# Values of the diagonal key tiles in two parts: the unmasked queries, then the 128 masked ones

## The chip, the cores and the metric

The kernel runs on one core of a Trainium2 chip. The metric is the time of one execution on the device, in microseconds (us). It is the median over several runs.

## What is computed

One transformer block on 2048 tokens of width 128: causal attention with 16 heads of width 8, a LayerNorm, then a feed-forward part with eight experts (each token goes to one) and a shared expert, and a second LayerNorm. The change touches the attention alone:

```python
y = x @ W.T + b                              # q, k, v; 16 heads of width 8
scores = einsum('bhqd,bhkd->bhqk', q, k) * scale
scores = where(k_pos > q_pos, -inf, scores)  # causal
p = softmax(scores - max(scores))
out = einsum('bhqk,bhkd->bhqd', p, v)
x = layernorm(x + out @ Wo.T + bo)
```

## The kernel before

**Tiles.** Queries are taken in four blocks B of 512 (`BLK`), keys in tiles j of 128 (`P`), heads in four groups g of four. A step s = 4B + g is one group of heads on one block of queries. Block B needs the key tiles 0 to 4B + 3. The last four of them, j >= 4B, lie on the diagonal: of tile 4B + d the first 128·d queries of the block see nothing, the next 128 see a triangle, and the rest see all. The first 128·d are never computed (`skip`).

**Two passes.** The *scores* pass finds each query's maximum: TensorE makes products in score_ps (two slots, L1263, and for the diagonal L1270 adds a mask), and VectorE reduces them (L1001). After the last piece of a step comes *maxima*: VectorE takes the maximum over the parts (L1009), GpSimd (POOL) splits it into three bf16 parts in five operations (L747, L752), TensorE turns them (L1278, `maxrows`), ScalarE copies them, and two DMAs lay them into q_stack as an extra row of the product. The second pass works on *quads*, one (g, j) with its four heads. For each quad there are two *probs* items (i = 0 and 1, two heads each): TensorE multiplies keys by queries into ring_ps (L1299), and ScalarE takes the exponential into probs (L876, one instruction a head). On a diagonal tile POOL then sets the forbidden corner of all four heads to zero, in one affine_select on their first 128 columns (L736), and counts `probs_masked` up. Then come the *values*: TensorE multiplies probs by v_aug into out_ps (L1319), which adds up over the key tiles; four matmuls, one a head, side by side in 32 columns of the array each. They are fp32, and the trace has eight records (and eight weight loads) for the four.

**Parts of the values.** The values of a quad can be issued in two parts, `first_values` and `values`. `columns` (L51) says which query columns each takes. Before the change it cuts them in the middle: 256 and 256 of an off-diagonal tile or of j = 4B (d = 0), 192 and 192 for d = 1. The tiles d = 2 (256 columns) and d = 3 (128 columns) are not cut. On a diagonal tile both parts wait for `probs_masked`; elsewhere they wait for `probs_ready`, the exponentials of the four heads.

**What sets the order.** `make_plan` (L61) writes one list of items, and each engine's program goes through it in that order, taking what concerns it. So every engine's queue is in the order of the plan. The second pass gives a fixed sequence (`main`): probs i = 0 of a quad, first_values of the quad before, probs i = 1, values of the quad before. Scores are put between them. The planner keeps a clock for TensorE, VectorE and ScalarE with estimated costs, and puts the next scores when they are due and would stand no longer than the item they go ahead of (L207 to L211). In it `exp_done` is the time at which a quad's probabilities can be used, 750 ns later for diagonal tiles (L171). Once all scores are issued, first_values items are dropped and the values are issued whole (L215). POOL's queue follows the same plan: its five operations of maxima, its masks (at probs i = 1 of the quad) and a `pow` for the LayerNorm (L757, at out_proj) stand there in plan order.

The lines that are spoken of most:

```python
1308                    if j >= TPB * B:
1309                        pe.wait_ge(probs_masked, TPB * s + j - TPB * B + 1)
1310                    else:
1311                        pe.wait_ge(probs_ready, 4 * k + 4)
```

## Time and profile before

| | |
|---|---|
| median of 3 runs | 598.13 us (597.97 to 601.04) |
| the profiled execution, own time | 595.15 us |
| its span, first to last instruction | 593.4 us |
| PE (TensorE matmuls) busy | 529.2 us (89%), 5257 records |
| DVE (VectorE) busy | 454.6 us (77%) |
| ACT (ScalarE) busy | 365.1 us (62%) |
| POOL (GpSimd) busy | 143.2 us (24%) |
| mean granted TensorE clock | 0.966 of full |

Busy time is the time in which an engine has an instruction at work. The profiled execution is a run of its own, 2.98 us below the median. The attention runs from about 22 us (first scores) to 496 us (last values); the last scores are issued at about 437 us. Between 437 and 496 us the second pass ends and is mixed with the first work of the experts; the rest is the experts and the output. "PE" is the matmul, "PEld" the load of its weights; an idle time in square brackets in a timeline row is that of the engine before that row, with what ended it.

### The profile page before, as it was taken

To read this page: it belongs to the slowest core of one execution; us is meant where nothing else is said; L and a number is where in the kernel's file an instruction comes from. 1 tells how busy PE (TensorE), PEld (TensorE's weight loads), DVE (VectorE), ACT (ScalarE), POOL (GpSimd) and SP (SyncE) were. 2 spreads that over 40 slices of the span, in tenths; PEclk is the share of its full clock that TensorE was granted. 3 is DMA by queue.
4 is the path that set the end of the run, shared out by engine and by line. 5 is a ranking of instruction groups with operands and counts; after the bars stand their busy time and mean duration, and the time that the engine had idled before them with its cause. 6 is when DMAs were issued, how large, how long until landed. Compare 5 with 4: busy or idle time off the path is not lost.

```text
span 593.4 us, 14002 instructions
## 1 busy us (share of the span) xinstructions
PE 529.2 (89%) x5257; PEld 218.2 (37%) x5257; DVE 454.6 (77%) x765; ACT 365.1 (62%) x805; POOL 143.2 (24%) x268
## 2 busy tenths in 40 slices
PE   5487899899798999989999999999998999998880
PEld 3243333333333333333333333333324225654460
DVE  4777999899876789888888879879854425777673
ACT  3035676467477666778787877777787984331450
POOL 4633311211201111010101002002013156224744
PEclk9669999899989999999999999999999999999995
DMA  6341002501000420001001000000001012211233
GB/s 152 106 111 54 2 3 58 143 17 31 1 28 2 121 68 2 30 1 29 2 1 29 2 9 21 2 3 2 1 2 36 24 33 56 44 57 34 48 66 93
DMA packets 28882, 22.60 MB, mean 38 GB/s; under 512 B 3528, under 2 KB 28048, under 8 KB 28816
## 3 DMA queue, kind: packets, MB, share of 16 engines
q1 hardware_dynamic: 26848, 18.43, 11.0%
q0 software_dynamic: 1536, 3.15, 3.1%
q8 instruction: 43, 0.70, 0.5%
q14 instruction: 23, 0.19, 0.1%
q10 hardware_dynamic: 432, 0.13, 0.1%
HBM read 8.00 MB, written 4.06 MB: 20 GB/s over the span
## 4 chain that ended last, share of the span: by engine, by line
PE 64%; DVE 12%; issue 6%; ACT 5%; POOL 5%; SPq 4%; DMA 2%; POOLq 0%; DVEq 0%; ACTq 0%
PE out_ps L1319 22%; PE ring_ps L1299 18%; PE score_ps L1263 10%; DVE part_max L1001 6%; SPq L620 3%; ACT probs L876 3%; PE score_ps L1410 3%; POOL probs L736 2%; PE ring_ps L1330 2%; PE ring_ps L1427 1%; PE score_ps L1299 1%; PE score_ps L1270 1%; POOL k_stack L816 1%; PE score_ps L1362 1%; ACT oT L890 1%
## 5 line engine op out<-in xcount | busy, mean ns | idle before, releaser
L1001 DVE TENSOR_REDUCE part_max<-score_ps 128x2 f32<-128x1024 f32 (+3 forms) x320 | 326.1, 1060 | 46.3 <-PE score_ps L1263 27.8
L876 ACT ACTIVATE probs<-ring_ps 128x512 f32<-128x512 f32 (+3 forms) x608 | 289.9, 531 | 113.8 <-PE ring_ps L1299 112.3
L1299 PE MATMUL ring_ps<-q_stack,k_stack 64*128 64x512 bf16 (+3 forms) x1216 | 179.1, 350 | 8.7 <-ACT probs L876 5.5
L1319 PE MATMUL out_ps<-probs,v_aug 128*32 128x256 f32 (+3 forms) x2144 | 174.1, 396 | 11.8 <-POOL probs L736 9.8
L1263 PE MATMUL score_ps<-k_stack,q_stack 64*128 64x512 bf16 (+3 forms) x640 | 119.8, 361 | 13.1 <-DVE part_max L1001 6.6
L1299 PEld LDWEIGHTS ring_ps<-q_stack,k_stack 64*128 64x128 bf16 x1216 | 54.0, 94 | 74.8 <-ACT probs L876 44.1
L736 POOL TENSOR_SCALAR_AFFINE_SELECT probs<-probs 128x512 f32<-128x512 f32 x64 | 40.7, 637 | 161.8 <-ACT probs L876 161.7
L1319 PEld LDWEIGHTS out_ps<-probs,v_aug 128*32 128x32 f32 x2144 | 43.0, 108 | 99.1 <-ACT probs L876 42.0
L1263 PEld LDWEIGHTS score_ps<-k_stack,q_stack 64*128 64x128 bf16 x640 | 34.0, 94 | 88.6 <-issue 41.3
L747 POOL CAST max_parts<-row_max 128x16 bf16<-128x16 f32 x48 | 9.6, 200 | 124.4 <-DVE row_max L1009 122.4
L803 POOL DMA_INDIRECT qk_parts<-xs_dram,q_stack x30 | 30.7, 1024 | 25.5 <-DVE q_stack L1128 17.7
L1270 PE MATMUL score_ps<-mask_wide,ident_wide 64*128 64x64 bf16 (+1 forms) x512 | 36.1, 215 | 0.0
L1410 PE MATMUL score_ps<-w_gu,qk_parts 128*128 x60 | 31.8, 613 | 0.0
L1270 PEld LDWEIGHTS score_ps<-mask_wide,ident_wide 64*128 64x128 bf16 x512 | 27.1, 100 | 10.7 <-issue 2.0
L757 POOL TENSOR_TENSOR rstd<-rstd,minus_half 128x1 f32<-128x1 f32 x16 | 8.9, 556 | 89.1 <-DVE rstd L959 89.1
L929 ACT ACTIVATE qk_parts<-score_ps 128x256 f32<-128x256 f32 x30 | 11.5, 384 | 28.5 <-PE score_ps L1410 27.9
L1146 DVE SCALAR_TENSOR_TENSOR qk_parts<-qk_parts,score_ps 128x256 f32<-128x256 f32 x30 | 12.6, 419 | 15.1 <-ACT qk_parts L929 14.9
L883 ACT ACTIVATE max_rows<-ring_ps 12x512 bf16<-12x512 f32 x15 | 8.7, 579 | 21.3 <-PE ring_ps L1278 21.2
L816 POOL DMA_INDIRECT k_stack<-sorted_dram,q_stack x16 | 16.8, 1049 | 15.4 <-DMA sorted_dram<-q_stack 10.7
L1427 PE MATMUL ring_ps<-wd,q_stack 128*128 x120 | 19.3, 284 | 0.2
L876 ACT ACTIVATE probs<-score_ps 128x512 f32<-128x512 f32 (+3 forms) x32 | 16.3, 544 | 1.6 <-PE ring_ps L1299 1.1
L1427 PEld LDWEIGHTS ring_ps<-wd,q_stack 128*128 128x128 f32 x120 | 15.7, 191 | 1.5 <-issue 0.8
(180 smaller groups left out, 403.6 us busy)
## 6 DMA issues: line engine op xcount, KB each, us to landing
q_stack<-qk_parts SPq DMA_DIRECT2D x36, 128.0 KB, 2.4
k_stack<-qk_parts SPq DMA_DIRECT2D x36, 128.0 KB, 2.4
sorted_dram<-q_stack SPq DMA_DIRECT2D x30, 64.0 KB, 1.5
x_sb<-in_L_attn_x_dram SPq DMA_DIRECT2D x4, 256.0 KB, 5.1
w_gu<-n_L_ffn_expert_gate_dram SPq DMA_DIRECT2D x8, 128.0 KB, 2.1
w_gu<-in_L_ffn_expert_up_dram SPq DMA_DIRECT2D x8, 128.0 KB, 2.2
wd<-n_L_ffn_expert_down_dram SPq DMA_DIRECT2D x8, 128.0 KB, 2.3
xs_dram<-qk_f SPq DMA_DIRECT2D x4, 256.0 KB, 2.3
```

What stands on the lines that cost most here:

```text
L620: sp.dma_start(to[p:P:HD, at, MAIN, :, :], parts).then_inc((q_stacked, k_stacked)[side][b], 16)
L736: pool.affine_select(out=square, in_=square, compare_op=ALU.is_ge, fill=0.0, base=0, pattern=[[0, 4], [1, P]], channel_multiplier=-1).then ...
L803: pool.indirect_dma_start(out=xg[:, k % 8, :], out_offset=None, in_=xs_dram[0:P * tiles[w][1], :], in_offset=bass.IndirectOffsetOnAxis(ap= ...
L816: pool.indirect_dma_start(out=yg[:, t, :], out_offset=None, in_=sorted_dram[w][:, :], in_offset=bass.IndirectOffsetOnAxis(ap=slot_i[:, t:t ...
L876: act.activation(probs[:, u % RING, 0:w], bank(("probs", u))[:, 0:w], ACT.Exp, scale=SCALE).then_inc(probs_ready, 1)
L1001: dve.tensor_reduce(out=part_max[:, s % 2, t, 2 * hp:2 * hp + 2, c], in_=score_ps[:, m % 2, :, 0:w], axis=AX.X, op=ALU.max).then_inc(score ...
L1263: last = mm(score_ps[:, m % 2, x, 0:w], q_stack[half, B % 2, MAIN, hh, t * P:(t + 1) * P], k_stack[half, c, MAIN, hh, 0:w], start=True, st ...
L1270: last = mm(score_ps[:, m % 2, x, w - P + skip:w], ident_wide[half, 64 + at:64 + at + P], mask_wide[half, at + skip:at + P], start=False, ...
L1299: last = mm(bank(unit)[:, 0:w], k_stack[half, j // TPB, rows, hh, keys], q_stack[half, B % 2, rows, hh, skip:BLK], start=rows == MAIN, sto ...
L1319: last = mm(out_ps[at:at + 32, lo:hi], v_aug[:, j, h * VC:h * VC + 32], probs[:, (4 * k + i) % RING, lo - skip:hi - skip], start=j == 0 an ...
L1410: mm(bank(it), xgT[:, k % 4, :], w_gu[:, bass.ds(e, 1), :].rearrange("p a n -> p (a n)"), start=True, stop=True).then_inc(gate_up_made, 1)
L1427: last = mm(bank(it)[:, 0:D], x_hidT[:, k % 2, f * P:(f + 1) * P], wd[:, bass.ds(e, 1), f, :].rearrange("p a n -> p (a n)"), start=f == 0, ...
```

## The change

`columns` now cuts a diagonal tile elsewhere. The first part takes the columns past the triangle (384, 256 and 128 of them for d = 0, 1 and 2), the second the 128 with the triangle. A first part exists for d = 0, 1 and 2, in the last stretch too, where off-diagonal tiles have none; d = 3 has only its 128 columns. The first part waits for the exponentials, the second for the mask. In the planner a first part's data are ready without the 750 ns, so the order of scores among the other items comes out another way.

```diff
     kind, quad, B, g, j = item
     skip = P * max(0, j - TPB * B)
-    middle = (skip + BLK) // 2
+    parts = ("first_values", *item[1:]) in plan
+    if j >= TPB * B:
+
+        masked = skip + P
+        return (masked, BLK) if kind == "first_values" else (skip, masked if parts else BLK)
+    middle = BLK // 2
     if kind == "first_values":
-        return skip, middle
-    return (middle if ("first_values", *item[1:]) in plan else skip), BLK
+        return 0, middle
+    return (middle if parts else 0), BLK
...
-                    if i == 0 and value[4] < TPB * value[2] + TPB // 2:
+                    if i == 0 and value[4] < TPB * (value[2] + 1) - 1:
                         main.append((("first_values", *value[1:]), due))
...
         if item[0] in ("first_values", "values"):
-            return max(clock["tensor"], exp_done[item[2:5]])
+            masked = item[0] == "values" and item[4] >= TPB * item[2]
+            return max(clock["tensor"], exp_done[item[2:5]] + 750 * masked)
...
-            exp_done[item[2:5]] = clock["scalar"] + 125 + (750 if item[4] >= TPB * item[2] else 0)
+            exp_done[item[2:5]] = clock["scalar"] + 125
...
-        if item[0] != "first_values" or job < len(jobs):
+        if item[0] != "first_values" or job < len(jobs) or item[4] >= TPB * item[2]:
             put(item)
...
                     lo, hi = columns(it, plan)
-                    if j >= TPB * B:
+                    first = kind == "first_values" or ("first_values", *it[1:]) not in plan
+                    if j >= TPB * B and kind == "values":
                         pe.wait_ge(probs_masked, TPB * s + j - TPB * B + 1)
                     else:
                         pe.wait_ge(probs_ready, 4 * k + 4)
...
                         last = mm(out_ps[at:at + 32, lo:hi], v_aug[:, j, h * VC:h * VC + 32],
-                                  probs[:, (4 * k + i) % RING, lo - skip:hi - skip], start=j == 0 and lo == 0, stop=j == TPB * (B + 1) - 1)
+                                  probs[:, (4 * k + i) % RING, lo - skip:hi - skip], start=j == 0 and first, stop=j == TPB * (B + 1) - 1)
```

The plan before has 108 first_values and 160 values items, that after 128 and 160. Of the 20 more, 14 are for d = 2 of the steps 0 to 13, and six for d = 0, 1, 2 of the steps 14 and 15, whose values are issued when no scores are left. The columns multiplied are the same in number.

The order of PE at an ordinary diagonal, step 9 (B = 2, g = 1), the values of d = 1 and d = 2. L1299 are probs (128x256 for d = 2, 128x128 for d = 3), L1263 and L1270 scores, L1319 values, one row for the four heads. Before:

```order
L1319 MATMUL out_ps<-probs,v_aug 32x192 x4
L1299 MATMUL ring_ps<-q_stack,k_stack 128x256 x4
L1319 MATMUL out_ps<-probs,v_aug 32x192 x4
L1263 MATMUL score_ps<-k_stack,q_stack 128x384 x2
L1270 MATMUL score_ps<-mask_wide,ident_wide 128x128 x2
L1270 MATMUL score_ps<-mask_wide,ident_wide 128x64 x2
L1299 MATMUL ring_ps<-q_stack,k_stack 128x128 x4
L1263 MATMUL score_ps<-k_stack,q_stack 128x512 x2
L1299 MATMUL ring_ps<-q_stack,k_stack 128x128 x4
L1319 MATMUL out_ps<-probs,v_aug 32x256 x4
```

With the change the same stretch (its lines are six or seven higher):

```order
L1326 MATMUL out_ps<-probs,v_aug 32x256 x4
L1269 MATMUL score_ps<-k_stack,q_stack 128x384 x2
L1276 MATMUL score_ps<-mask_wide,ident_wide 128x128 x2
L1276 MATMUL score_ps<-mask_wide,ident_wide 128x64 x2
L1305 MATMUL ring_ps<-q_stack,k_stack 128x256 x4
L1326 MATMUL out_ps<-probs,v_aug 32x128 x4
L1269 MATMUL score_ps<-k_stack,q_stack 128x384 x2
L1276 MATMUL score_ps<-mask_wide,ident_wide 128x128 x2
L1276 MATMUL score_ps<-mask_wide,ident_wide 128x64 x2
L1305 MATMUL ring_ps<-q_stack,k_stack 128x128 x4
L1326 MATMUL out_ps<-probs,v_aug 32x128 x4
L1269 MATMUL score_ps<-k_stack,q_stack 128x512 x2
```

The 192 and 192 columns of d = 1 are now 256 and 128, and the 256 columns of d = 2 two groups of 128, the first of them between the two probs of d = 3.

The second place is where maxima stand right ahead of a mask in POOL's queue late in a diagonal. PE before, step 6 (B = 1, g = 2), with the maxima of step 8 behind the L1263 and L1270 of the first rows:

```order
L1263 MATMUL score_ps<-k_stack,q_stack 128x512 x2
L1270 MATMUL score_ps<-mask_wide,ident_wide 128x128 x2
L1270 MATMUL score_ps<-mask_wide,ident_wide 128x64 x2
L1299 MATMUL ring_ps<-q_stack,k_stack 128x256 x4
L1319 MATMUL out_ps<-probs,v_aug 32x192 x4
L1299 MATMUL ring_ps<-q_stack,k_stack 128x128 x8
L1263 MATMUL score_ps<-k_stack,q_stack 128x512 x2
L1319 MATMUL out_ps<-probs,v_aug 32x256 x4
```

With the change it is step 5 (B = 1, g = 1) that has this sequence, with the maxima of step 7:

```order
L1269 MATMUL score_ps<-k_stack,q_stack 128x512 x2
L1276 MATMUL score_ps<-mask_wide,ident_wide 128x128 x2
L1276 MATMUL score_ps<-mask_wide,ident_wide 128x64 x2
L1305 MATMUL ring_ps<-q_stack,k_stack 128x256 x4
L1326 MATMUL out_ps<-probs,v_aug 32x128 x4
L1305 MATMUL ring_ps<-q_stack,k_stack 128x128 x4
L1326 MATMUL out_ps<-probs,v_aug 32x128 x4
L1305 MATMUL ring_ps<-q_stack,k_stack 128x128 x4
L1269 MATMUL score_ps<-k_stack,q_stack 128x512 x2
L1326 MATMUL out_ps<-probs,v_aug 32x128 x4
```

At step 6 the maxima of step 8 now come after the diagonal. POOL's queue shows the same; there, before, around the maxima of step 7 and on to the mask behind them:

```order
L747 CAST max_parts<-row_max 128x8x2
L752 TENSOR_TENSOR row_max<-row_max,max_parts 128x4x2x2
L747 CAST max_parts<-row_max 128x8x2
L752 TENSOR_TENSOR row_max<-row_max,max_parts 128x4x2x2
L747 CAST max_parts<-row_max 128x8x2
L736 AFFINE_SELECT probs<-probs 128x4x128
L757 TENSOR_TENSOR rstd<-rstd,minus_half 128x1
L736 AFFINE_SELECT probs<-probs 128x4x128 x2
```

and with the change, from the pow to the masks of d = 2 and d = 3:

```order
L763 TENSOR_TENSOR rstd<-rstd,minus_half 128x1
L753 CAST max_parts<-row_max 128x8x2
L758 TENSOR_TENSOR row_max<-row_max,max_parts 128x4x2x2
L753 CAST max_parts<-row_max 128x8x2
L758 TENSOR_TENSOR row_max<-row_max,max_parts 128x4x2x2
L753 CAST max_parts<-row_max 128x8x2
L742 AFFINE_SELECT probs<-probs 128x4x128 x2
```

The maxima of step 7 moved from ahead of the mask of d = 1 to ahead of that of d = 2.

## Rows read from the trace of the kernel before

**Rows 1.** Windows: engines by stage, us busy; columns as in the first line.

```profile
core 0: us, PE busy (x) PEld busy (x) DVE busy (x) ACT busy (x) POOL busy (x), PEclk, DMA share, GB/s
0.00:59.00 59.00, 38.94 (x401) 20.15 (x403) 41.59 (x66) 20.22 (x46) 25.14 (x57) 0.83 0.41 106
59.00:120.00 61.00, 55.58 (x647) 22.27 (x645) 56.13 (x73) 38.37 (x90) 13.38 (x30) 0.97 0.19 54
120.00:437.00 317.00, 303.88 (x3374) 108.06 (x3370) 270.20 (x331) 229.48 (x475) 39.04 (x89) 0.99 0.07 18
437.00:496.00 59.00, 55.85 (x462) 20.42 (x462) 21.32 (x78) 47.35 (x109) 22.05 (x45) 1.00 0.10 27
```

**Rows 2.** Waits, 120 to 437 us: us in total, times, longest us.

```profile
DVE part_max L1001 <- PE score_ps L1263: 25.2, 44, 2.5
PE out_ps L1319 <- POOL probs L736: 6.3, 11, 3.0
PE ring_ps L1299 <- ACT probs L876: 3.1, 8, 0.5
PE score_ps L1263 <- DVE part_max L1001: 1.2, 3, 0.5
```

**Rows 3.** Timeline at 256 us, step 9, d = 1 (start us, us, engine, line ...).

```profile
255.00 0.87 ACT L876 ACTIVATE probs<-ring_ps 128x384 f32<-128x384 f32 x2 [0.87 <-PE ring_ps L1299]
...
255.94 0.64 POOL L736 TENSOR_SCALAR_AFFINE_SELECT probs<-probs 128x512 f32<-128x512 f32 x1 [2.10 <-ACT probs L876]
...
256.08 0.25 PE L1270 MATMUL score_ps<-mask_wide,ident_wide 64*128 64x128 bf16 x4
...
256.63 0.53 PE L1319 MATMUL out_ps<-probs,v_aug 128*32 128x192 f32 x8 [0.30 <-POOL probs L736]
...
257.42 0.53 PE L1319 MATMUL out_ps<-probs,v_aug 128*32 128x192 f32 x8
```

**Rows 4.** Timeline of PE at 62 to 96 us: groups of values, and what follows them.

```profile
62.91 0.43 PE L1319 MATMUL out_ps<-probs,v_aug 128*32 128x128 f32 x8
63.27 0.50 PE L1299 MATMUL ring_ps<-q_stack,k_stack 64*128 64x384 bf16 x4
...
94.29 0.25 PE L1270 MATMUL score_ps<-mask_wide,ident_wide 64*128 64x128 bf16 x4
94.47 0.64 PE L1319 MATMUL out_ps<-probs,v_aug 128*32 128x256 f32 x8
95.04 0.28 PE L1263 MATMUL score_ps<-k_stack,q_stack 64*128 64x256 bf16 x2
95.16 0.25 PE L1270 MATMUL score_ps<-mask_wide,ident_wide 64*128 64x128 bf16 x4
95.24 0.60 PE L1299 MATMUL ring_ps<-q_stack,k_stack 64*128 64x512 bf16 x4
```

**Rows 5.** Timeline at 158 to 165 us, step 6, d = 2.

```profile
158.02 2.35 DVE L1001 TENSOR_REDUCE part_max<-score_ps 128x2 f32<-128x1024 f32 x2
...
159.30 0.39 PE L1263 MATMUL score_ps<-k_stack,q_stack 64*128 64x512 bf16 x2
...
160.40 0.20 DVE L1009 TENSOR_REDUCE row_max<-part_max 128x16 f32<-128x48 f32 x1
...
160.68 0.24 POOL L747 CAST max_parts<-row_max 128x16 bf16<-128x16 f32 x1 [1.94 <-DVE row_max L1009]
...
161.99 1.23 POOL L736 TENSOR_SCALAR_AFFINE_SELECT probs<-probs 128x512 f32<-128x512 f32 x2
...
162.69 0.64 PE L1319 MATMUL out_ps<-probs,v_aug 128*32 128x256 f32 x8 [3.00 <-POOL probs L736]
...
164.51 1.23 DVE L1001 TENSOR_REDUCE part_max<-score_ps 128x2 f32<-128x1024 f32 x1 [2.51 <-PE score_ps L1263]
```

**Rows 6.** Windows: an ordinary stretch, the wait of step 6, and after it.

```profile
90.00:93.00 3.00, 3.00 (x44) 1.23 (x40) 2.40 (x4) 2.73 (x6) 0.15 (x1) 1.00 0.00 0
160.00:163.00 3.00, 0.31 (x8) 0.16 (x8) 1.96 (x4) 0.00 (x0) 2.03 (x7) 1.00 0.00 0
163.60:167.00 3.40, 3.40 (x24) 1.08 (x20) 1.23 (x1) 2.39 (x5) 0.00 (x0) 0.50 0.00 0
```

**Rows 7.** Waits, 0 to 120 us.

```profile
PE out_ps L1319 <- POOL probs L736: 1.8, 4, 0.9
```

**Rows 8.** Timeline at 450 us, step 14, d = 1, no scores left.

```profile
450.00 0.64 POOL L736 TENSOR_SCALAR_AFFINE_SELECT probs<-probs 128x512 f32<-128x512 f32 x1
...
450.69 0.85 PE L1319 MATMUL out_ps<-probs,v_aug 128*32 128x384 f32 x8 [0.62 <-POOL probs L736]
```

**Rows 9.** The page, part 5: the values over the whole run.

```profile
L1319 PE MATMUL out_ps<-probs,v_aug 128*32 128x256 f32 (+3 forms) x2144 | 174.1, 396 | 11.8 <-POOL probs L736 9.8
```

## The prediction

> **What bounds the kernel now.** I read the stages first, then the waits, then the rows around single waits. By stage [rows 1]: from 120 to 437 us PE is busy 303.88 of 317 us (96%), DVE 270.20 (85%), ACT 229.48 (72%). So in more than half of the run TensorE sets the pace. From 437 to 496 us it is the same: PE 55.85 of 59 us, DVE 21.32. From 59 to 120 us PE (55.58 of 61) and DVE (56.13) are level, and before 59 us the kernel starts up and nobody is full. The reader is to see that a microsecond of PE counts fully behind 120 us, and hardly before it.
>
> The waits of 120 to 437 us [rows 2] say what PE loses there: 6.3 us in 11 waits of the values for the mask, the longest 3.0 us; 3.1 us for ACT; only 1.2 us for DVE. In turn DVE stood 25.2 us waiting for PE's scores, so it has room when PE goes faster. The mask waits are the largest item that the change touches, but small: 1% of the run.
>
> **A short wait and what removes it.** Step 9, d = 1 [rows 3]: the last exponentials of the quad end at 255.87 us (255.00 + 0.87), the mask runs from 255.94 to 256.58, and the values start at 256.63. The matmuls ahead of them started at 256.08. In an ordinary place the same succession (scores' mask matmuls, then values) takes 0.18 us from start to start, 94.29 to 94.47 [rows 4], so they could have started at 256.26. They lost 0.37 us where the row shows 0.30 of idle time; I add 0.08 to each shown wait. With the change this first part waits for the exponentials alone, which were done 0.39 us before 256.26: nothing is left to wait for. The masked part comes behind another probs item and mostly scores. Here the second half already started at 257.42, 0.84 us after the mask had ended, and the masked part stands at the same place. So a usual mask is covered.
>
> The ten short waits of this stage come to 6.3 - 3.0 = 3.3 us, with 0.08 each to 4.1 us. Bounds: 3.3 us if the idle time is all, 4.1 as above, and 0 if all of it comes back as another wait. I take **-4.1**, since the rows around the wait show nothing next in line.
>
> **What an additional group costs.** The columns are the same; 20 groups of four heads are new. A group of 128 columns takes 0.36 us until the next item starts (62.91 to 63.27), one of 256 takes 0.57 (94.47 to 95.04) [rows 4]. So 128 columns are 0.21 us and 0.15 us are fixed. Going into values from scores takes 0.18 us (94.29 to 94.47), going into probs instead 0.08 (95.16 to 95.24): 0.10 more. A group costs 0.15 + 0.10 = **0.25 us**. Bounds: 0 where it stands in a wait, 0.36 (the whole row) if nothing of its columns were saved at the other part; I take 0.25, from neighbouring rows of the same shapes.
>
> The Trainium skill ("TensorE: Matmul & The Clock Gate", section "Back-to-back issue gap") gives an isolated matmul a fixed part of about 2.5 ns on top of its columns at the full clock. By that the eight records of a group would be an estimated 0.02 us, and the change would cost next to nothing. The 0.15 us between the two groups speaks against it, and the measured rows decide.
>
> Where the 20 groups stand: 9 of the 14 for d = 2 lie between 120 and 437 us (steps 5 to 13), 5 before 120 us (steps 0 to 4), and 6 behind 437 us (steps 14 and 15). One of the nine stands inside a long wait (next part). The other eight are paid: **+2.0**.
>
> **The long wait.** At step 6, d = 2 [rows 5], the mask did not wait for its exponentials but stood in POOL's queue behind the maxima of step 8: DVE finishes its two reductions at 160.37, the maximum is taken at 160.40, POOL's five operations start at 160.68, the masks at 161.99, and the values at 162.69 after 3.00 us of idle PE. Everything behind the values on PE stood too, among it the next scores, so DVE in turn was idle for 2.51 us until 164.51. After it the granted clock was 0.50 from 163.6 to 167.0 us, the 1.2 GHz level, where 90 to 93 us shows 1.00; from 160 to 163 us PE had done 0.31 us of work [rows 6]. 3.40 us at half rate are up to 1.7 us lost.
>
> The planner has moved this, not removed it. The orders above show the same sequence at step 5 with the maxima of step 7: scores, maxima, probs, second part of d = 1, two probs of d = 3, scores, and the masked part of d = 2. New is only that the 128 unmasked columns of d = 2 go ahead of the wait. They take 0.21 + 0.25 = 0.46 us out of it, leaving some 2.5 us, and 128 columns fewer are left behind it. Net **-0.2**, and the slow clock stays. At step 6 the wait is gone.
>
> **The other stages.** From 437 to 496 us six groups are 6 × 0.25 = 1.5 us. Their gain: at step 14, d = 1 [rows 8] the values wait 0.62 us, which the first part removes (0.7 with the 0.08); **+0.8**. d = 3 still waits for its mask whole. Before 120 us the waits for masks are 1.8 us in 4 [rows 7], against 5 × 0.25 = 1.25 us of new groups. With DVE as full as PE there, I take **0**; bounds -2.1 (all waits with their 0.08, groups covered) and +1.25 (nothing gained, all paid).
>
> Moved items: ACT, POOL and SP issue the same instructions, in another order by a few places. The maxrows items (one copy and two small DMAs each) move with the scores; the DMAs have tens of microseconds until their step. I cost this at nothing, covered by DVE's 25.2 us; if maxima or a copy came late for a step's first probs, a few tenths each.
>
> **Sum.** -4.1 + 2.0 - 0.2 + 0.8 + 0 = **-1.5 us**. The profiled execution took 595.15 us (span 593.4), so it would be 593.65. The median of the runs is 2.98 us higher; against it I forecast 598.13 - 1.5 = **596.6 us**. A difference below 0.5% (3.0 us) can hardly be told from none in this kernel.
>
> **The rivals.**
>
> *The waits change their name (slower).* PE, no longer held by masks, runs into the ring buffers (3.1 us of waits for ACT already) or into DVE's two score slots [rows 2]. The 4.1 and 0.7 us come back there, and 14 groups × 0.25 = 3.5 us are paid in full: 598.13 + 3.5 - 0.2 = 601.4 us, and 602.7 if the first 120 us pay their 1.25 as well. It decides from 1.5 us on that return, of the 4.8; beyond 0.5% it takes nearly all. For it: POOL ended the short waits only 0.37 us late, and ACT is the next on the path of every probs. Against it: DVE's 85% and ACT's 72%. Chance 0.17.
>
> *The long wait goes away (faster).* If DVE happens to be less behind at step 5, the maxima are done before the mask is wanted: 2.5 us and the slow stretch's 1.7 are gained, and the hidden group is paid (0.25): 596.6 - 3.95 = 592.7 us. For it: DVE's backlog differs from place to place. Against it: the order before the wait is alike row by row, and DVE is fuller near 130 us. Chance 0.17.
>
> *A second long wait.* Another maxima meets a late part of a diagonal: 2.5 + 1.7 = 4.2 us, 600.8 us. In POOL's order no other stands so; 0.05.
>
> *The cut is nearly free.* If the fixed part hides behind the array's other work, costs fall away: -4.1 - 0.2 - 0.7 = -5.0, 593.1 us. This is the result nearest to the skill's rule above. The 0.15 us in the rows speaks against it; 0.05.
>
> *The change does nothing.* If the first parts waited as long as before, for exponentials that end no earlier than the mask, all cost and no gain would be left, the time of the first rival. The 0.07 us between the exponentials' end and the mask's start, and the mask's own 0.64, exclude it where the queue is free. It has 0.01, within the first rival's time.
>
> **How the numbers follow.** The forecast case has 0.55, with a spread of its own of some 2.5 us to either side, since each of its terms rests on an order that is new as a whole: 594 to 599. The five others are as above. Below 595.14 us (faster by over 0.5%): the long wait's 0.17, the free cut's 0.05, and 0.12 of the forecast's lower edge: 0.34. Above 601.12: most of the first rival, 0.13, half of the second long wait, 0.02, and 0.03 of the forecast: 0.18. The rest, 0.48, is within. The range that holds it 8 times in 10 reaches to the fast rival and to the first slow one: 592.2 to 601.0.
>
> **What would show it.** In the profile after: PE has 160 more records, 5417. The waits for the mask in the values' line fall from 9.8 us [rows 9] to some 4 (the long one of about 2.5 near 135 us, and d = 3). One half-clock stretch follows it and the one near 163 us is gone. Waits of PE for DVE and ACT between 120 and 437 us stay below 6 us together. The stretch from the last scores to the last values grows by 0.8 us. The prediction is wrong if the waits for ACT or DVE grow by what the mask's lose, if a group of 128 columns takes other than 0.36 us, or if a wait of over 1 us stands where the order showed none.

## The result: 591.18 us, 1.1% faster, and the profile after

| | before | after |
|---|---|---|
| median (4 runs each) | 598.05 us (597.62 to 601.04) | 591.18 us (589.64 to 593.04) |
| ratio | | 0.9887, 95% interval 0.9847 to 0.9927 |
| profiled execution, own time | 595.15 us | 591.83 us |

The forecast was 596.6 us with a range from 592.2: the sign was right, the size not. The gain is between 4.4 and 9.2 us by the interval, where 1.5 was forecast. The two profiled executions are 3.3 us apart; that of before was quicker than its median. From the page of the profile after, its span and busy times:

```profile
span 590.1 us, 14322 instructions
PE 531.4 (90%) x5417; PEld 222.9 (38%) x5417; DVE 454.6 (77%) x765; ACT 365.4 (62%) x805; POOL 143.0 (24%) x268
```

PE has the 160 more records that were expected. By stage, the columns those of [rows 1]:

```profile
0.00:59.00 59.00, 39.27 (x381) 20.17 (x381) 39.52 (x63) 19.21 (x44) 24.41 (x56) 0.80 0.40 106
59.00:120.00 61.00, 55.00 (x693) 22.90 (x695) 55.35 (x72) 39.33 (x92) 14.57 (x33) 1.00 0.17 47
120.00:437.00 317.00, 308.28 (x3493) 112.50 (x3491) 274.92 (x335) 233.28 (x482) 40.68 (x101) 0.99 0.07 19
437.00:496.00 59.00, 57.12 (x492) 21.66 (x488) 21.40 (x82) 45.18 (x105) 22.16 (x34) 0.97 0.12 32
```

PE is busier from 120 to 437 us, 308.28 us against 303.88 [rows 1]. The stages themselves have moved: the last scores start at 431.7 us, 4.8 us earlier than before (436.5), and the last values at 492.2 against 495.5. So the gain arises before the last scores, and 1.5 us of it are lost again between them and the last values. From 60 us to the last scores, before and after:

```profile
60.00:436.50 376.50, 358.25 (x4002) 129.56 (x3999) 324.83 (x401) 266.96 (x560) 51.78 (x118) 0.99 0.09 24
60.00:431.70 371.70, 358.37 (x4142) 133.94 (x4136) 326.93 (x404) 267.91 (x563) 51.90 (x119) 0.99 0.09 24
```

PE's busy time is the same. Its idle time, the stretch less the busy time, fell from 18.25 to 13.33 us, and that is the whole of the 4.8 us. The waits from 120 to 437 us, against [rows 2]:

```profile
DVE part_max L1007 <- PE score_ps L1269: 19.6, 40, 1.5
PE out_ps L1326 <- POOL probs L742: 3.0, 1, 3.0
PE ring_ps L1305 <- ACT probs L882: 2.5, 7, 0.5
PE score_ps L1269 <- DVE part_max L1007: 1.2, 3, 0.6
```

Of the waits for the mask one is left, the long one; the ten short ones (3.3 us) are gone, and what PE waited for ACT and DVE in these rows did not grow. At step 9, d = 0 and then d = 1, the rows are as the change draws them; [rows 3] has the same step, d = 1, before:

```profile
251.89 0.64 POOL L742 TENSOR_SCALAR_AFFINE_SELECT probs<-probs 128x512 f32<-128x512 f32 x1 [1.49 <-ACT probs L882]
...
252.06 0.85 PE L1326 MATMUL out_ps<-probs,v_aug 128*32 128x384 f32 x8
...
253.28 0.42 PE L1326 MATMUL out_ps<-probs,v_aug 128*32 128x128 f32 x8
...
253.63 0.39 PE L1269 MATMUL score_ps<-k_stack,q_stack 64*128 64x512 bf16 x2
...
254.30 0.64 PE L1326 MATMUL out_ps<-probs,v_aug 128*32 128x256 f32 x8
254.32 0.63 POOL L742 TENSOR_SCALAR_AFFINE_SELECT probs<-probs 128x512 f32<-128x512 f32 x1 [1.79 <-ACT probs L882]
```

The first part of d = 0 (384 columns, 252.06) starts while the mask of its own tile is still at work (251.89 to 252.53), and its masked part at 253.28 finds it done. That part takes 0.35 us until the scores at 253.63. The first part of d = 1 (256 columns, 254.30) starts before its mask (254.32) does.

The long wait has moved to step 5, as the order said; against [rows 5] and [rows 6]:

```profile
132.80 2.35 DVE L1007 TENSOR_REDUCE part_max<-score_ps 128x2 f32<-128x1024 f32 x2
...
134.07 0.39 PE L1269 MATMUL score_ps<-k_stack,q_stack 64*128 64x512 bf16 x2
...
135.18 0.18 DVE L1015 TENSOR_REDUCE row_max<-part_max 128x16 f32<-128x32 f32 x1
...
135.44 0.24 POOL L753 CAST max_parts<-row_max 128x16 bf16<-128x16 f32 x1 [1.92 <-DVE row_max L1015]
...
136.74 1.23 POOL L742 TENSOR_SCALAR_AFFINE_SELECT probs<-probs 128x512 f32<-128x512 f32 x2
...
137.44 0.66 PE L1326 MATMUL out_ps<-probs,v_aug 128*32 128x128 f32 x8 [2.97 <-POOL probs L742]
```

```profile
134.30:137.30 3.00, 0.17 (x2) 0.00 (x0) 2.42 (x4) 0.29 (x2) 1.58 (x6) 0.87 0.00 0
136.50:143.40 6.90, 5.96 (x39) 2.21 (x40) 3.17 (x5) 2.59 (x5) 1.41 (x4) 0.51 0.00 0
```

It was to shrink from 3.00 to 2.5 us and is 2.97. The half-clock stretch is 6.9 us long, twice that of step 6 before. It is not the only one. Between 45 and 578 us the changed kernel has two more (the first two rows), and the kernel before has one beside that of step 6 (the third row):

```profile
51.20:54.60 3.40, 3.40 (x34) 1.66 (x30) 2.52 (x3) 2.71 (x6) 0.63 (x1) 0.50 0.01 4
454.00:457.40 3.40, 3.40 (x19) 0.67 (x14) 2.04 (x10) 2.05 (x5) 0.98 (x4) 0.50 0.24 77
109.00:112.40 3.40, 3.40 (x24) 1.44 (x21) 2.68 (x5) 0.72 (x3) 0.84 (x4) 0.51 0.67 185
```

Together that is 13.7 us at the lower clock after the change and 6.8 us before it: the changed kernel is faster although its clock is lower for longer. The one at 51.2 us follows two waits of over 1 us, of PE's values for the mask (1.27 us at 48.22, where one of 0.87 stood before) and of probs for the DMA that places the maxima (0.84 before):

```profile
50.05 0.61 PE L1305 MATMUL ring_ps<-q_stack,k_stack 64*128 64x512 bf16 x4 [1.40 <-DMA q_stack<-max_rows]
```

The rows of the weight loads (PEld) show further waits. The loads are issued ahead of their matmuls, and a row of theirs can show a wait where the matmul's own gap is under the 0.15 us from which gaps are listed. Over the whole run, before:

```profile
PEld score_ps L1263 <- DVE part_max L1001: 34.7, 85, 1.3
PEld out_ps L1319 <- POOL probs L736: 18.2, 28, 3.3
```

and after:

```profile
PEld score_ps L1269 <- DVE part_max L1007: 29.4, 67, 1.4
PEld out_ps L1326 <- POOL probs L742: 7.4, 5, 3.3
PE out_ps L1326 <- POOL probs L742: 5.9, 4, 3.0
```

The mask waits on PE fell from 9.8 us [rows 9] to 5.9, where some 4 were forecast: of the rest, 2.2 us stand before 120 us, where it was 1.8 before. The loads for the scores waited 34.7 us for DVE before and 29.4 after: 5.3 us less. The prediction had not read this row, and costed the order of the scores at nothing. A load can wait while the matmuls ahead of it still work, so its waits are not time lost by themselves; the experiments show how little this row says of the time.

### The profile page after: what moved, and what is told of

Same layout as the page of the kernel before. It is cut to its first block, busy times and chain, and to the rows that moved or that the text cites. A ratio compares the mean times of both kernels' runs of the same rounds, so it can differ in the third digit from the quotient of the medians.

```text
span 590.1 us, 14322 instructions
## 1 busy us (share of the span) xinstructions
PE 531.4 (90%) x5417; PEld 222.9 (38%) x5417; DVE 454.6 (77%) x765; ACT 365.4 (62%) x805; POOL 143.0 (24%) x268
## 4 chain that ended last, share of the span: by engine, by line
PE 69%; DVE 12%; issue 5%; POOL 5%; ACT 4%; SPq 2%; DMA 2%; POOLq 0%; DVEq 0%; ACTq 0%
PE out_ps L1326 24%; PE ring_ps L1305 19%; PE score_ps L1269 10%; DVE part_max L1007 5%; PE score_ps L1417 3%; SPq L626 2%; ACT probs L882 2%; PE ring_ps L1337 2%; PE score_ps L1305 2%; PE ring_ps L1434 1%; PE score_ps L1276 1%; PE ring_ps L1236 1%; POOL k_stack L822 1%; ACT oT L896 1%; PE score_ps L1369 1%
## 5 line engine op out<-in xcount | busy, mean ns | idle before, releaser
L1326 PE MATMUL out_ps<-probs,v_aug 128*32 128x256 f32 (+3 forms) x2304 | 179.1, 382 | 7.9 <-POOL probs L742 5.9
L1326 PEld LDWEIGHTS out_ps<-probs,v_aug 128*32 128x32 f32 x2304 | 46.2, 108 | 97.2 <-ACT probs L882 47.8
L822 POOL DMA_INDIRECT k_stack<-sorted_dram,q_stack x16 | 16.8, 1049 | 15.3 <-DMA sorted_dram<-q_stack 10.6
```

The costliest lines, as they stand in the source:

```text
L822: pool.indirect_dma_start(out=yg[:, t, :], out_offset=None, in_=sorted_dram[w][:, :], in_offset=bass.IndirectOffsetOnAxis(ap=slot_i[:, t:t ...
L1326: last = mm(out_ps[at:at + 32, lo:hi], v_aug[:, j, h * VC:h * VC + 32], probs[:, (4 * k + i) % RING, lo - skip:hi - skip], start=j == 0 an ...
```

## The experiments

All ratios are to the kernel before, run in turn on the same chip. One percent is 6 us. r1 to r4 ran on one chip, r5 to r8 on a second, r9 to r12 on a third and r13 to r15 on a fourth; from one of these groups to another the ratios are to be compared rather than the medians. "Theory" and its letter stand for what the expectation of a run names so. The edits that the tables need:

| run | cut and waits | order | masks in POOL's queue | median us | ratio (95% interval) |
|---|---|---|---|---|---|
| r1 | new | new | as planned | 591.48 | 0.9897 (0.9862 to 0.9933) |
| r2 | new cut, all wait | new | as planned | 608.07 | 1.0178 (1.0142 to 1.0215) |
| r3 | old | new | as planned | 600.44 | 1.0059 (1.0031 to 1.0088) |
| r4 | new | old | as planned | 595.22 | 0.9970 (0.9941 to 0.9998) |
| r5 | new cut, all wait | old | as planned | 604.95 | 1.0135 (1.0108 to 1.0162) |
| r6 | new | third | as planned | 592.31 | 0.9914 (0.9888 to 0.9941) |
| r7 | new, not d = 2 | fourth | as planned | 594.35 | 0.9941 (0.9914 to 0.9967) |
| r8 | new, not in the last stretch | new | as planned | 592.06 | 0.9917 (0.9885 to 0.9948) |
| r9 | new | new | ahead of maxima | 586.27 | 0.9819 (0.9791 to 0.9846) |
| r10 | old | old | ahead of maxima | 592.90 | 0.9922 (0.9900 to 0.9944) |
| r11 | old | old, planned with 650 ns | as planned | 595.18 | 0.9960 (0.9938 to 0.9982) |
| r12 | old | old, planned with 850 ns | as planned | 596.59 | 1.0002 (0.9980 to 1.0024) |
| r13 | new | old | ahead of maxima | 590.58 | 0.9879 (0.9841 to 0.9917) |
| r14 | new | third | ahead of maxima | 596.83 | 0.9985 (0.9959 to 1.0011) |
| r15 | new | new | eight items ahead | 594.11 | 0.9937 (0.9905 to 0.9968) |

The kernel before had medians of 595.87 to 597.98 us on the four chips (17 to 23 runs on each).

**r1: the changed kernel once more.**

> The changed kernel once more, against the kernel before on the same chip. Theory A (the gain of the medians, 6.9 us, is real and the two profiled executions, 3.3 us apart, understate it because that of before was a fast one): the medians are 6 to 8 us apart again. Theory B (the gain is the 3.3 us of the profiles, the rest is the spread of a few runs): 2.5 to 4.5 us.

0.9897 after 0.9887. By the ratio that is 6.1 us, inside theory A; by the medians (595.87 and 591.48) it is 4.4 us, inside theory B. The run does not decide between them. Two profiled executions of this one program differ by 2.2 us in their span, and on PE most of the difference shows at one place. First the quicker one, then the other:

```profile
32.34 0.59 PE L1284 MATMUL ring_ps<-ident_wide,max_parts 128*12 128x128 bf16 x4 [0.20 <-POOL max_parts L753]
```

```profile
34.56 0.58 PE L1284 MATMUL ring_ps<-ident_wide,max_parts 128*12 128x128 bf16 x4 [1.97 <-POOL max_parts L753]
```

The same matmul waits 0.20 us for POOL's maxima in one execution and 1.97 in the other, and everything behind it is 2.2 us later. The delay comes from further back: POOL fills q_stack (L710) before its maxima, behind DVE's work on the queries and keys, and starts that at 20.47 us in one and 22.68 in the other. Why DVE was later there was not followed. Spans of single executions are to be compared with that in mind; the profile of before has the quick start.

**r2: the new cut and order, but every part waits for the mask.**

```diff
-                    if j >= TPB * B and kind == "values":
+                    if j >= TPB * B:
```

> The changed kernel with its order and its cut, but every part of a diagonal tile waits for the mask. Theory W (the first parts' freedom from the mask is what gains): it loses the 4.8 us that the prediction priced, or more, and lands within 2 us of the kernel before. Theory O (the new order of the scores gains, the waits only a little): it stays within 2 us of the changed kernel.

16.6 us slower than the changed kernel: theory W's direction, and more than three times the 4.8 us that were priced. It was to land within 2 us of the kernel before, and is 1.8% slower:

```profile
PE out_ps L1326 <- POOL probs L742: 22.2, 33, 3.9
```

33 waits of 22.2 us together, against 6.0 us in r1: the 16.2 us between them are nearly the whole difference in time. The kernel before has 17 waits of 9.8 us [rows 9]. The prediction priced the freedom by the waits of the old cut. With the new cut there are more first parts (d = 2 has one), and each stands in front of its mask.

**r3: the old cut and waits in the new order.**

```diff
+    last = max(n for n, it in enumerate(plan) if it[0] == "scores")
+    plan = [it for n, it in enumerate(plan) if it[0] != "first_values" or (n < last and it[4] < TPB * it[2] + TPB // 2)]
...
-                    lo, hi = columns(it, plan)
+                    lo, hi = cut(it, plan)
-                    if j >= TPB * B and kind == "values":
+                    if j >= TPB * B:
```

(`cut` is the old `columns`.)

> The old cut (halves, none for d = 2, none in the last stretch) and the old waits, in the order that the changed planner makes. Theory O: 3 to 7 us faster than the kernel before. Theory W: no faster than the kernel before, and slower by a few us, since the planner now counts on first parts that are ready early, and PE meets the waits head on.

Slower than before, 1.0059, as theory W had it, so the new order is no good for the old values:

```profile
PEld score_ps L1281 <- DVE part_max L1019: 29.7, 69, 1.4
PE out_ps L1338 <- POOL probs L754: 13.7, 21, 3.0
```

It has the smaller wait of the loads for DVE (29.7 us), as the changed kernel has, and is the slower kernel all the same. Its mask waits are 13.7 us against 9.8, and its trace has 13.7 us at half clock between 60 us and the last scores, where the kernel before has 6.8.

**r4: the new cut and waits in the old order.**

```diff
+    for it in [it for it in plan if it[0] == "values" and TPB * it[2] <= it[4] < TPB * it[2] + TPB - 1]:
+        if ("first_values", *it[1:]) not in plan:
+            at = max(n for n, x in enumerate(plan[:plan.index(it)]) if x[0] == "probs")
+            plan.insert(at, ("first_values", *it[1:]))
```

> The new cut and the new waits, in the old order (the 20 new first parts are put right ahead of the second probs of the next quad). Theory W: 2 to 7 us faster than the kernel before, most of the gain of the change. Theory O: within 2 us of the kernel before, as 4.7 us of new groups and some 4.8 us of waits cancel.

0.9970 is 1.8 us, the forecast's 1.5 within its interval (and inside theory O's 2 us). The mask's waits are gone as in the changed kernel, but PE waits more for DVE:

```profile
PEld score_ps L1282 <- DVE part_max L1020: 36.6, 88, 1.4
PE score_ps L1282 <- DVE part_max L1020: 9.1, 23, 1.2
PE out_ps L1339 <- POOL probs L755: 5.2, 4, 3.0
60.00:435.80 375.80, 359.27 (x4092) 131.04 (x4089) 324.55 (x401) 267.10 (x560) 51.79 (x118) 0.99 0.09 24
```

PE's mask waits fell by 4.6 us (9.8 to 5.2), and its waits for DVE rose by 2.5 (6.6 to 9.1), while those for ACT fell from 5.5 to 4.6: net, about a third of what the cut gains comes back under another name in this order. From 60 us to the last scores PE is idle for 16.5 us, between the 18.25 of before and the 13.33 of the changed kernel. So cut and waits by themselves give as much as was priced, and the rest of the gain, 0.9970 to 0.9897 or some 4 us, comes with the order. Neither theory had this: the two are not additive. The order costs 0.6% with the old values (r3) and gains 0.7% with the new ones.

**r5: as r4, and every part waits for the mask.** The same edit of the wait as in r2, on r4.

> The new cut in the old order, with every part of a diagonal tile waiting for the mask: 20 groups more and no freedom. Against the same order with the new waits (595.2 us in the run before this one), the difference is the worth of the freedom in the old order: 4.8 us by the prediction. Against the kernel before, the cost of the cut by itself: 20 x 0.25 = 5.0 us at most, 3.5 us if the first 120 us hide theirs. If instead the freedom is worth as much here as in the new order (16.6 us there), it comes out over 610 us.

8.7 us over the kernel before, more than the 5.0 us that were expected at most, and 9.7 us over r4 (9.8 by the ratios), twice the 4.8. Its waits for the mask are 18.5 us:

```profile
PE out_ps L1339 <- POOL probs L755: 18.5, 30, 4.0
```

The groups' own cost cannot be read from this run, since the cut makes 8.7 us of waits besides (18.5 against 9.8).

**r6: the planner counts the mask for first parts.**

```diff
-            masked = item[0] == "values" and item[4] >= TPB * item[2]
+            masked = item[4] >= TPB * item[2]
```

> The changed kernel, but its planner still counts the 750 ns of the mask for first parts; cut and waits are the new ones. If the planner's knowledge that first parts are ready early makes the 4 us which the new order brings over the old one (591.5 against 595.2 us), it lands near 595 us or above. If any order that is planned with the additional items does as well, it stays within 1.5 us of 591.5 us.

592.31 us and 0.9914, within 1.5 us of the changed kernel: it isn't the planner's knowledge of early first parts. But it is as quick in another way:

```profile
PEld score_ps L1269 <- DVE part_max L1007: 44.7, 90, 1.3
PE out_ps L1326 <- POOL probs L742: 0.8, 1, 0.8
PE ring_ps L1284 <- POOL max_parts L753: 2.0, 1, 2.0
```

```profile
45.00:578.00 533.00, 503.02 (x5220) 205.09 (x5216) 420.71 (x697) 354.37 (x784) 116.78 (x218) 1.00 0.12 31
```

The loads for the scores wait 44.7 us for DVE, 15.3 more than in the changed kernel; in turn its maxima stand so that no long wait arises, and from 45 to 578 us the granted clock is 1.00.

**r7: no first part for d = 2.**

```diff
-                    if i == 0 and value[4] < TPB * (value[2] + 1) - 1:
+                    if i == 0 and value[4] < TPB * (value[2] + 1) - 2:
```

> The changed kernel without first parts for d = 2 (its 256 columns whole, behind the mask), 16 groups fewer. By the price of 0.25 us a group, 11 paid of them, 2.7 us less work; against it the waits for the mask of d = 2, which before were 0.2 to 0.3 us each in the rows, and a whole second long wait. I expect 0 to 2 us faster than the changed kernel; slower by more than 2 us would say that d = 2 is where the cut pays.

A miss: 594.35 us, where 0 to 2 us less than the changed kernel were expected. On the same chip r6 and r8 have 592.3 and 592.1. The ratios of r7 and r8, 0.9941 and 0.9917, have intervals that overlap, so that the first parts of d = 2 pay is suggested and not shown. The loads for the values waited for the mask 12 times against 5, but the order differs here too, and the profiled execution (598.00 us) is the slowest of twelve.

**r8: no first parts in the last stretch.** `or item[4] >= TPB * item[2]` is taken out of the planner's last condition.

> The changed kernel without first parts in the last stretch (six groups fewer; the order up to the last scores is the same). The prediction had the last stretch 0.8 us longer by them: so 0.8 us faster than the changed kernel, within 0.5 us; the same or slower would say that the groups there cost less than 0.25 us or that more than one wait of 0.7 us went.

0.9917 against 0.9887 and 0.9897 of the changed kernel: no difference that can be told. The order up to the last scores is the same, and the two profiled executions, both with the quick start, have spans of 589.8 and 590.1 us. From the last scores to the last values they take 60.0 and 60.5 us. So the six groups cost 0.5 us there at most as the traces have it, and not clearly anything.

**r9: masks ahead of maxima in POOL's queue, in the changed kernel.**

```diff
+            pool_plan = list(plan)
+            for n, it in [(n, it) for n, it in enumerate(plan) if it[0] == "maxima"]:
+                near = plan[n + 1:n + 1 + MASKS_AHEAD]
+                until = next((m for m, x in enumerate(near) if x == ("maxrows", it[1]) or x[0] == "maxima"), len(near))
+                masks = [x for x in near[:until] if x[0] == "probs" and x[5] == 1 and x[4] >= TPB * x[2]]
+                for x in masks:
+                    pool_plan.remove(x)
+                at = pool_plan.index(it)
+                pool_plan[at:at] = masks
-            for it in plan:
+            for it in pool_plan:
```

with MASKS_AHEAD = 3.

> The changed kernel, but in POOL's queue a mask that stands within three items behind the maxima goes ahead of them (PE's order is the same). Theory L (the long wait near 137 us and the half clock after it cost what their rows show): 3.0 us of wait and up to 3.4 us of the 6.8 us at half clock are saved, 4.5 to 6.5 us faster than the changed kernel, some 586 us. Theory D (DVE's score slots take the place of any wait of PE before 190 us): half of it or less, 589 us or more.

586.27 us, as theory L had it. The mask of step 5, d = 2 now runs as soon as its exponentials are there, and PE does not stand:

```profile
134.14 0.43 PE L1336 MATMUL out_ps<-probs,v_aug 128*32 128x128 f32 x8
...
134.16 0.63 POOL L752 TENSOR_SCALAR_AFFINE_SELECT probs<-probs 128x512 f32<-128x512 f32 x1
```

```profile
130.00:137.00 7.00, 6.83 (x90) 3.12 (x86) 6.71 (x12) 3.43 (x11) 2.46 (x7) 1.00 0.01 2
136.50:143.40 6.90, 6.12 (x67) 2.51 (x63) 6.40 (x9) 5.43 (x11) 1.35 (x5) 1.00 0.20 59
```

The second of these windows, 136.5 to 143.4 us, had a granted clock of 0.51 in the changed kernel and has 1.00 here. This version is quicker than both kernels.

**r10: the same in the kernel before.**

> The same in the kernel before: the wait of 3.0 us near 163 us and 3.4 us at half clock. Theory L: 3.5 to 5 us faster than the kernel before. Theory D: 2.5 us or less. If both this and the run before it gain alike, the long wait had no part in the difference between the two kernels.

0.9922, 4.6 us: theory L. r9 against r1 is 0.9819 against 0.9897, 4.7 us by the ratios. The edit gains alike in both, so the long wait has no visible part in their difference. It is not the long wait alone that the edit touches: here maxrows, which come behind the maxima, now wait 2.6 us for them in four waits, where PE had no such wait before.

**r11, r12: another figure for the mask in the planner of the kernel before.**

```diff
-            exp_done[item[2:5]] = clock["scalar"] + 125 + (750 if item[4] >= TPB * item[2] else 0)
+            exp_done[item[2:5]] = clock["scalar"] + 125 + (650 if item[4] >= TPB * item[2] else 0)
```

> The kernel before, whose planner counts 650 ns for a mask instead of 750; nothing else. Another order by some 276 places. Theory S (any new order scatters by a few us through DVE's slots and the places of the maxima, so the 4 us that the new order brought are one draw): 1.5 to 5 us away from the kernel before, to either side. Theory P (only planning for the additional items gains): within 1.5 us of it.

> The kernel before with 850 ns in the planner: some 74 places differ, and maxima stand before the same masks as they did. Theory S: 0.5 to 3 us away, to either side. Theory P: within 1.5 us.

0.9960 and 1.0002: 2.4 us and nothing. The first is inside theory S, the second outside it (0.5 to 3 us). An order that is new in 276 places moves the time by 0.4%, which is over half of what the changed kernel's order gives. In r11 the longest wait for the mask is 1.6 us: its order has no long wait, and is only 2.4 us faster.

**r13: r4 with the masks ahead.**

> The new cut and waits in the old order, with the masks ahead of the maxima in POOL's queue, so that the long wait stands in neither of what is compared. Against the kernel before with the masks ahead (592.9 us), the difference is what cut and waits are worth by themselves; against the changed kernel with the masks ahead (586.3 us), what the order is. If the order is worth 4 us or more without the long wait: 590 to 592.5 us. If the long wait and the slow clock behind it (6.8 us in the old order too) were what differed: 586 to 588 us.

590.58 us, in the range for an order that is worth 4 us by itself. Against r10 (0.9922) cut and waits are 0.4%, 2.6 us; against r9 (0.9819) the order is 0.6%, 3.6 us by the ratios and 4.3 by the medians. The loads' waits for DVE are 36.8 us in the old order and 31.6 in the new, with no long wait in either. From 60 us to the last scores, r13 and then r9:

```profile
60.00:430.20 370.20, 356.81 (x4101) 130.92 (x4097) 324.10 (x401) 266.92 (x560) 51.68 (x119) 1.00 0.09 24
60.00:428.20 368.20, 357.11 (x4127) 133.51 (x4126) 326.86 (x405) 267.71 (x563) 52.05 (x119) 1.00 0.09 25
```

PE is idle for 13.4 us in the old order and 11.1 in the new.

**r14: r6 with the masks ahead.**

> The changed kernel whose planner counts the mask for first parts (592.3 us), with the masks ahead in POOL's queue. Its trace had no long wait and no half clock between 45 and 578 us, and some 10 us more of waits for DVE at the scores than the changed kernel. If that reading holds, there is nothing for the masks to gain: 592 us within 1.5. If it falls by 4 us or more as the other two did, the reading is wrong.

596.83 us: not within 1.5 of 592. It did not fall, so that half of the reading of r6 stands, but it rose by 4.5 us (0.9914 to 0.9985, 4.2 us), which I had not expected. In this order the masks that go ahead make the maxima late, and TensorE's maxrows wait for them, 5.1 us in 5 waits; in r6 it was one of 2.0, that of the start:

```profile
PE ring_ps L1294 <- POOL max_parts L763: 5.1, 5, 2.0
```

And a half clock that r6 had not follows, from 114.4 us on:

```profile
114.40:121.20 6.80, 6.44 (x52) 2.76 (x52) 4.51 (x11) 3.20 (x7) 2.01 (x3) 0.50 0.65 176
```

Beside r13 this run says something about orders too. Both have the new cut and waits and the masks ahead, on one chip, and the third order, planned with the additional items, is 6.2 us slower than the old one (596.83 against 590.58).

**r15: masks up to eight items ahead.**

> The changed kernel with masks up to eight items behind the maxima ahead of them, the mask of d = 3 at step 5 among them. Its wait for the mask of d = 3 there goes, but the maxima of step 7 come some 3 us later, with its maxrows behind. Within 1.5 us of the version with three items (586.3 us); slower by 2 us or more if the maxima's lateness is what bites.

594.11 us, 7.8 us slower than with three (7.0 by the ratios). The lateness of the maxima bites, in the first steps above all:

```profile
PE ring_ps L1294 <- POOL max_parts L763: 7.5, 4, 2.2
```

```profile
63.30:73.50 10.20, 9.61 (x80) 3.54 (x80) 5.28 (x6) 4.99 (x12) 1.46 (x3) 0.50 0.01 3
```

7.5 us of waits in all, the later three at 44, 64 and 86 us, and a half clock of 10.2 us from 63.3 us on.

## Why the prediction was right and wrong

**The short waits (-4.1).** Right in the trace of the changed kernel: ten of 3.3 us of idle time gone, nothing put in their place in the PE rows of that stage. In the old order it was not so: in r4 2.5 us of waits for DVE came up where 4.6 us of mask waits went. As the worth of the freedom it was mis-sized: r4 against r5 gives 9.7 us and r1 against r2 16.6 us. The waits of the old cut are not those that the new cut would have. (The 0.08 us added to each wait is 0.07 by its own rows, 0.37 less 0.30; that changes the sum by 0.1 us.)

**A group's cost (0.25).** The row came out as read: a group of 128 columns takes 0.35 us until the next item (253.28 to 253.63), 0.36 was read before. What one group more costs the kernel was measured by no run alone. With the mask's gain it made -1.5 us, and r4, which has these terms alone, measured -1.8 us (-0.1 to -3.5 by its interval; r13 against r10: -2.6). The sum agrees, its terms do not: PE's waits for the mask, DVE and ACT together came down by 3.0 us in r4 and not by 4.1, and 3.4 us more stood at half clock. That r4 lands so near the forecast is in part luck.

**The long wait (-0.2).** Its place was right, its length not: 2.97 us, where some 2.5 were forecast. The wait hangs on the chain that starts with DVE's last two reductions: from their start over the maxima on POOL and the mask to PE's values it is 4.67 us before (158.02 to 162.69, [rows 5]) and 4.64 after (132.80 to 137.44). The scores before the wait start 1.28 us behind DVE in one kernel (159.30) and 1.27 in the other (134.07), so the group put ahead only filled time before them. The rival that the wait would vanish did not happen; its price of 4.2 us (2.5 + 1.7) is near the 4.6 and 4.7 us of r10 and r9, an edit that changes more than this one wait.

**The last stretch (+0.8).** It grew by 1.5 us, from 59.0 (436.5 to 495.5) to 60.5 us (431.7 to 492.2). That the groups did it is not shown: without them (r8) it is 60.0 us, and the changed kernel and r8 both have 3.4 us at half clock there, which the kernel before has not.

**The first 120 us (0).** One of the forecast's own signs of being wrong came up here: two waits of over 1 us where the order showed none, and a half clock behind them. That "the DMAs have tens of microseconds until their step" does not hold at the start, where probs waited for that DMA in both kernels (0.84 and 1.40 us).

**The step that failed: "Moved items ... I cost this at nothing".** Old against new order, with the new cut and waits, is 0.9970 against 0.9897 (r4, r1: 595.2 and 591.5 us) and 0.9879 against 0.9819 (r13, r9: 590.6 and 586.3 us): about 4 us both times, and the missing part of the gain. By the intervals each of the two is uncertain by an estimated 2.8 us, so they show a gain and not its size. The prediction called it "covered by DVE's 25.2 us", the time in which DVE stood waiting for PE. What the runs show in place of nothing is less idle time of PE between 60 us and the last scores: 16.5 us in r4 and 13.3 in the changed kernel, 13.4 in r13 and 11.1 in r9. PE's waits for DVE at the scores and for ACT at the probs make over half of it: in that stretch they are 5.5 and 4.1 us in r4, 4.0 and 3.1 in the changed kernel; 4.9 and 4.1 in r13, 4.6 and 3.1 in r9. The stage's weight loads for the scores had 18.1 us of waits for DVE before, where I had read "1.2 us for DVE" from the PE row [rows 2]. That DVE's slots press more than the 1.2 us say is right. But the loads' row prices nothing: it is 29.7 us in r3, which is slower than before, 30.5 in r1, and 44.7 in r6, which is as fast as r1.

**The slow rival** (the waits change their name) is excluded for this order: the kernel is faster, and PE's waits for DVE at the scores and for ACT at the probs are 10.2 us over the whole run (7.1 and 3.1) against 12.1 before (6.6 and 5.5). In the old order (r4) it happened in part. **The cheap cut** would have given 593.1 us. The figure that the prediction took for it from the Trainium skill ("TensorE: Matmul & The Clock Gate", section "Back-to-back issue gap") is that of an isolated matmul; the same section says that it under-counts a stream of weight loads and matmuls with few columns (its example has 128). That the measured time is near 593.1 us is no support: the row still shows 0.35 us for 128 columns, and the cut by itself (r4), which was to gain 5.0 us by this rival, gains 1.8 us and by its interval at most 3.5.

**Open.** Why this order suits the new cut is not settled. Planning with the additional items is no rule for it: two orders so planned gained (r1, r6), but with the masks ahead one of them gained over the old order (r9) and the other lost 6.2 us to it (r14, r13). Two orders planned without them gained 0.4% and nothing (r11, r12). So the order's 4 us can be a lucky draw; it is measured, but no rule was shown by which the next one would have it. Nor is it shown why the medians of the two kernels lie further apart than their profiled executions; the start of r1 shows that 2.2 us of it can come from the start alone. What the half-clock stretches cost by themselves was not measured either; they come and go with the order.

## What to carry to other kernels

Where a planner or a greedy scheduler sets the order, a change of its costs is a change of everything behind it: run the new work in the old order first, then the new order, and don't put the sum down to the edit. Price a freed wait by the waits that the new shape would have without the freedom, not by those of the old one. And when one wait of a few microseconds stands in a queue behind work that nobody needs yet, try another order of that queue, and measure it: here it gave both kernels some 4.6 us, nearly as much as the change, but the same edit cost 4 us in the order of r6, where no long wait stood, and going eight items ahead instead of three lost it all again.

## What the runs showed of the hardware

Three things I had not expected. A PE row of waits can say 1.2 us where the weight loads of the same line say 18.1. The two are to be read together, but the loads' row is no price: from r1 to r6 it rose from 30.5 to 44.7 us at the same time within the intervals.

One wait of 3 us was followed by 3.4 us at half clock in the kernel before [rows 6] and by 6.8 us in r4, at the same wait of step 6 and with the same 3.0 us on PE:

```profile
163.90:170.70 6.80, 6.54 (x46) 2.19 (x49) 3.89 (x4) 4.62 (x9) 0.00 (x0) 0.51 0.14 41
```

The granted clock fell to the 1.2 GHz level after TensorE had stood, and the length of the stretch was not fixed by the length of the wait.

And two executions of one program differed by 2.2 us in their span. It shows on PE as one wait (0.20 against 1.97 us) near 33 us. Two single traces can be this far apart without any change of the program.
